# Four graph layers on one core: in layers 1 and 3 the edge work goes by tile with its results kept in a ring for the per-slot sums; in layer 0 the record fields are loaded once

## The reference

```
L0: alpha = softmax over the edges of a src of leaky(s_i[src] + s_j[dst]); sum alpha * (x W)[src] by dst
L1: g = attr64 @ Wdesc.T;  agg_i = sum over edges of node i=src of g * ssp(x Wj.T)[dst]
    m = ssp(x Wi.T) + agg; three residual MLPs, u*x + (...), two more residual MLPs
L2: z = relu(layernorm(x[src] @ top + x[dst] @ bottom)) * weight; mean by dst; gated update
L3: W = ssp(attr50 @ w1.T + b1) @ w2.T + b2, times a cosine cutoff C
    agg_i = sum over edges of node i=src of W*C * (x lin1.T)[dst];  x = x + ssp(agg @ lin2.T + b)
```

## Time and profile before

| | |
|---|---|
| median of the runs | 6994.6 us |
| profiled execution: span, its own time | 8544.4 us; the profile gives no second time for it |
| PE, DVE, ACT, POOL busy over the span | 4906.1, 4571.7, 2591.3, 4414.8 us |
| l0d, l1e, l3e in the profiled execution | 1363.7, 1400.5, 1434.9 us |
| DMA | 541.31 MB, mean 63 GB/s |

### The profile page before, as it was taken

The page is one execution under the profiler, slowest core; times in us unless marked ns, Lnnn a source line. Parts: engine busy times, 40 slices in busy tenths (PEclk is TensorE's granted clock), DMA queues, the critical chain, the costliest instruction groups (busy, mean ns, idle before and its releaser), DMA issues. The chain is left out here.

```text
span 8544.4 us, 129169 instructions
## 1 busy us (share of the span) xinstructions
PE 4906.1 (57%) x25390; PEld 3718.7 (44%) x25391; DVE 4571.7 (54%) x14726; ACT 2591.3 (30%) x6676; POOL 4414.8 (52%) x4764
## 2 busy tenths in 40 slices
PE   6666666622444444663454545656666556777767
PEld 4444444411333333552443444234444444555554
DVE  8655555534444444664333334867667674555555
ACT  2333333301212223663000000833333343333333
POOL 0255555544666665555555555046666615555553
PEclk9866676755555556776656566878788876776776
DMA  1233333351111112442222222022222212222221
GB/s 51 69 102 102 102 104 103 100 45 36 48 48 48 48 48 75 117 101 49 59 61 59 58 59 55 0 57 65 64 65 65 64 33 58 54 54 55 54 54 43
DMA packets 858703, 541.31 MB, mean 63 GB/s; under 512 B 652277, under 2 KB 757577, under 8 KB 858185
## 3 DMA queue, kind: packets, MB, share of 16 engines
q1 hardware_dynamic: 710536, 239.88, 12.9%
q0 software_dynamic: 148032, 300.00, 12.9%
HBM read 411.68 MB, written 127.68 MB: 63 GB/s over the span
## 5 line engine op out<-in xcount | busy, mean ns | idle before, releaser
L1326 POOL DMA_INDIRECT l2e_rows<-l_rows,k_src_of x832 | 841.9, 1012 | 749.8 <-POOLq L215 329.7
L1326 POOL DMA_INDIRECT spare<-l_rows,k_dst_of x832 | 804.9, 967 | 742.2 <-DVE l3e_prod L2313 311.5
L813 POOL DMA_INDIRECT src_records<-sort_rec,sort_idx x784 | 761.4, 971 | 767.8 <-DVEq L706 515.3
L1326 POOL DMA_INDIRECT l1e_rows<-l_rows,k_dst_of x832 | 785.8, 944 | 641.1 <-issue 296.7
L1193 POOL DMA_INDIRECT dst_rows<-l0d_out,l0d_idx x832 | 820.5, 986 | 466.7 <-issue 246.8
L866 DVE TENSOR_TENSOR acc<-acc,l1e_pR 128x128 f32 x832 | 238.6, 287 | 886.8 <-remote 703.5
L1494 PE MATMUL l1e_pG<-k_weights,l1e_dT 64*128 64x128 f32 x1664 | 233.7, 426 | 696.1 <-ACT l1e_dT L1514 412.0
L2247 PE MATMUL l3e_pH<-l3e_dT,k_weights 50*128 50x256 f32 x832 | 380.0, 549 | 341.0 <-DMA run_ml<-h_nodes 327.0
L2155 PE MATMUL l2e_pR<-l2e_z,l2e_oh 128*128 128x128 f32 x1664 | 301.0, 337 | 464.1 <-DVE acc L866 309.4
L1160 PE MATMUL l0d_pX<-table,l0d_ohT 128*128 x1664 | 448.9, 448 | 154.7 <-issue 71.2
L1494 PEld LDWEIGHTS l1e_pG<-k_weights,l1e_dT 64*128 64x128 f32 x1664 | 176.9, 292 | 771.4 <-issue 397.3
(11 more groups left out here) (413 smaller groups left out, 13714.8 us busy)
## 6 DMA issues: line engine op xcount, KB each, us to landing
sort_rows<-lo_rows SPq DMA_DIRECT2D x196, 256.0 KB
sort_rec<-rec SPq DMA_DIRECT2D x98, 472.0 KB
l0m_rows<-dst_rows SPq DMA_DIRECT2D x416, 66.0 KB, 2.1
l0m_rows<-dst_rows POOLq DMA_DIRECT2D x416, 66.0 KB
l1e_rec<-src_records SPq DMA_DIRECT2D x832, 32.0 KB
l2e_lrow<-dst_local SPq DMA_DIRECT2D x208, 128.0 KB
l3e_rec<-src_records SPq DMA_DIRECT2D x832, 25.0 KB
l0d_meta<-src_records SPq DMA_DIRECT2D x832, 6.0 KB
```

Of the source, the lines that this page charges most:

```text
L813: e.indirect_dma_start(kn.by_src_rec[:, :], bass.IndirectOffsetOnAxis(ap=r["idx"][:, st.quad, j:j + 1], axis=0), r["rec"][:, st.quad, j, : ...
L1326: e.indirect_dma_start(r["rows"][:, i % ring, j, 0:width], None, table[:, :], bass.IndirectOffsetOnAxis(ap=columns[:, i * G + j:i * G + j ...
```

## The change

- **l1e and l3e.** Gathers, record loads, products and all before them go by tile: `TSTEPS` = 196 steps instead of 208. `prod` becomes a ring of `KEEP` = 16 steps (64 tiles). Only the one-hots, the sum products and the additions still go by slot, in 208 steps; `add` on PE reads from the new table `kept_reg` which tile of the ring each slot wants. A stage can now have its own number of steps, and `run_steps` goes on with it after the others have ended.
- The four record loads of a step become one DMA of four tiles.
- The operands of the sum product change sides, so that its result is [node, feature]. l1e adds into `MT`, cleared at its start; mlp's first layer becomes a transposition on PE and an addition to `AC`. l3c is written anew: transpose `AC`, copy on ACT, product, bias, clamp, Exp, Ln, max, add, without the transposition back.
- **l0d.** SP loads the 12 fields of all 784 tiles in eight DMAs at the start into the arrays of sums (not in use yet); for each slot ACT copies its 12 values to `meta` (four small copies a step). `dst_of` is written once at the end, by tile, and the arrays of sums are cleared after it.
- Some small tiles move to other places in SBUF; the work in them stays.

The diff, cut to its core (`...` stands for what is left out):

```diff
+TSTEPS = T // G
+KEEP = 16
@@ run_steps
+    total = max(t[1] + (t[3] if len(t) > 3 else n) for t in stages)
...
-    for r in range(n, n + lag):
+    for r in range(n, total):
         one(r)
+def wait_tiles(eng, sem, st):
+    eng.wait_ge(sem, min(st.i + 1, TSTEPS) if isinstance(st.i, int) else st.i + 1)
@@ offsets
+            ch(e.tensor_scalar(kn.kept_reg[:, :], kn.slot_reg[:, :], KEEP * G - 1, None, ALU.bitwise_and))
@@ add_stages, hot_stages
-    return [(stage(j), lag) for j in range(G)]
+    return [(stage(j), lag, 1, STEPS) for j in range(G)]
@@ l0_messages: sync
-                tiles = slot_values(kn, e, kn.slot_regs["sync"], st, 64)
-                wait_step(e, r["msg_ok"], st, RING)
-                for j in range(G):
-                    e.dma_start(r["meta"][:, st.ring, j, :], kn.by_src_rec[bass.ds(tiles[j] * P, P), CM:CM + META]
-                                ).then_inc(r[f"ld{st.ring}"], 16)
+            for c in range(8):
+                e.dma_start(fields[:, c * part:(c + 1) * part, :], rows[:, c * part:(c + 1) * part, CM:CM + META]
+                            ).then_inc(r[f"ld{c}"], 16)
+            ready = [(c + 1) * part // G for c in range(7)] + [STEPS]
+            for c in range(8):
+                e.wait_ge(r[f"ld{c}"], 16)
+                e.sem_inc(r["loaded"], ready[c] - (ready[c - 1] if c else 0))
@@ l0_messages: vector
-            ch(e.memset(kn.sums0[:, :], 0.0))
-            ch(e.memset(kn.odd[:, :], 0.0))
...
-                ch(e.tensor_copy(kn.dst_of[:, slots], meta[:, :, 4]))
...
+            ch(e.tensor_copy(kn.dst_of[:, :], fields[:, :, 4]))
+            ch.wait()
+            ch(e.memset(kn.both[:, :], 0.0))
@@ l0_messages: scalar
+            def meta(st):
+                tiles = slot_values(kn, e, kn.slot_regs["scalar"], st, 64)
+                wait_step(e, r["loaded"], st)
+                wait_step(e, r["msg_ok"], st, RING)
+                for j in range(G):
+                    ins = e.activation(r["meta"][:, st.ring, j, :], whole[:, bass.ds(tiles[j] * META, META)], ACT.Copy)
+                ins.then_inc(r["meta_ok"], 1)
+            run_steps(e, ch, [(meta, 0), (exp, 5), (rows, 3), (copy, 1)], STEPS, RING)
@@ soft_layers (mlp's first layer has w == "turn")
+                    for j in range(GROUPS):
+                        ins = e.transpose(r["p"][:, m % 4, j // 4, (j % 4) * P:(j % 4 + 1) * P],
+                                          lay.src[:, GROUPS * (i % NW) + j, :], kn.ident[:, :])
@@ load_records
+        e.dma_start(r["rec"][:, st.quad, :, 0:width], rows[:, bass.ds(st.i * G, G), column:column + width]
+                    ).then_inc(r[f"ld{st.quad}"], 16)
+def kept_tile(r, at):
+    return r["prod"][:, bass.ds(at * P, P)]
+def kept_step(r, st):
+    return r["prod"][:, bass.ds((st.i % KEEP) * (G * P), G * P)]
+def kept_values(kn, e, st):
+    regs = kn.slot_regs["tensor"]
+    e.load(regs, kn.kept_reg[64:65, bass.ds(st.i * G, G)])
+    return [e.snap(g, min_val=0, max_val=KEEP * G - 1) for g in regs]
@@ l1_edges (l3_edges alike: 196 steps, add and hot with 208)
             def add(st):
+                kept = kept_values(kn, e, st)
                 wait_step(e, r["hot"], st)
-                wait_step(e, r["prod_ok"], st)
+                wait_tiles(e, r["prod_ok"], st)
                 wait_step(e, r["added"], st, 2)
                 for j in range(G):
-                    ins = e.matmul(r["pR"][:, st.par, j, :], r["prod"][:, st.par, j, :], r["oh"][:, st.par, j, :],
+                    ins = e.matmul(r["pR"][:, st.par, j, :], r["oh"][:, st.par, j, :], kept_tile(r, kept[j]),
                                    start=True, stop=True)
-            run_steps(e, ch, [(mults, 1), (add, 3), (turn_rec, 0)], STEPS, QUAD)
+            run_steps(e, ch, [(mults, 1), (add, 3, 1, STEPS), (turn_rec, 0)], TSTEPS, QUAD)
...
-                wait_step(e, r["summed"], st, 2)
+                wait_step(e, r["summed"], st, 4)
...
-            run_steps(e, ch, in_turn(add_stages(kn, e, ch, r, 1, 6), hot_stages(kn, e, ch, r, 1, 4, 2, 2))
-                      + [(prod, 4)], STEPS, RING)
+            ch(e.memset(kn.MT[:, :, :], 0.0))
+            ch.wait()
+            run_steps(e, ch, in_turn(add_stages(kn, e, ch, r, 1, 6, kn.MT), hot_stages(kn, e, ch, r, 1, 4, 2, 2))
+                      + [(prod, 4)], TSTEPS, RING)
@@ l3_finish (new vector order; its other engines follow it)
+            for k in range(GROUPS + 3):
+                if k < GROUPS:
+                    keep(k)
+                if 0 < k <= GROUPS:
+                    bias(k - 1)
+                if 1 < k < GROUPS + 2:
+                    smooth(k - 2)
+                if 0 < k <= GROUPS:
+                    clamp(k - 1)
+                if k > 2:
+                    add(k - 3)
```

More of the change, by code:

```diff
@@ L104, in one @@
             c, size = r - t[1], (t[2] if len(t) > 2 else 1)
-            if c % size or (k is None and not 0 <= c < n):
+            if c % size or (k is None and not 0 <= c < (t[3] if len(t) > 3 else n)):
                 continue
@@ L113, in one @@
                                       i % 4, i % RING, (unroll // RING) * k + i // RING))
-            t[0](steps if len(t) > 2 else steps[0])
+            t[0](steps if size > 1 else steps[0])
     if n < first + 2 * unroll:
-        for r in range(n + lag):
+        for r in range(total):
             one(r)
@@ L864, in add @@
                 ch.until(last[0])
-            acc = block(kn, kn.AC, blocks[j])
+            acc = block(kn, into, blocks[j])
             ins = e.tensor_tensor(acc, acc, r["pR"][:, st.par, j, :], ALU.add)
@@ L1099, in local_a @@
             def local_a(st):
[L1100 removed]
+                wait_step(e, r["meta_ok"], st)
                 slots, meta = bass.ds(st.i * G, G), r["meta"][:, st.ring, :, :]
@@ L1316, in l0_sums, with gather_rows @@
                     + [f"{m}{j}" for m in ("ld", "ld_first") for j in range(RING)])
-def gather_rows(kn, e, r, table, width, columns, used, ring=4):
-    for i in range(STEPS):
+def gather_rows(kn, e, r, table, width, columns, used, ring=4, steps=STEPS):
+    for i in range(steps):
         if i >= ring:
@@ L1651, in build @@
     def build(r):
+        small, at = spare[:, 7 * SLOTS:], 0
+        for name, size in (("none", NB), ("less", 1), ("log_var", NB), ("std0", NB), ("shift0", NB), ("mv0", 2 * NB)):
+            r[name] = small[:, at:at + size]
+            at += size
+        r["mv0"] = r["mv0"].rearrange("p (b c) -> p b c", c=2)
         def pick(name, k):
@@ L2401, in scalar @@
                 if k < GROUPS:
-                    e.wait_ge(r["clamped"], k + 1)
-                    ch(e.activation(r["part"][:, k % 2, :, :], r["part"][:, k % 2, :, :], ACT.Exp))
-                if k < GROUPS:
+                    for q in halves(k):
+                        e.wait_ge(r["turned"], q + 1)
+                        if q > 3:
+                            e.wait_ge(r["product"], q - 3)
+                        e.activation(r["T"][:, q % 4, 0:len(members(q)), :], four(r["pA"], q), ACT.Copy
+                                     ).then_inc(r["copied"], 1)
+                if k:
+                    e.wait_ge(r["clamped"], k)
+                    t = r["part"][:, (k - 1) % 2, :, :]
+                    ch(e.activation(t, t, ACT.Exp))
                     ch.wait()
-                    e.activation(r["part"][:, k % 2, :, :], r["part"][:, k % 2, :, :], ACT.Ln, bias=kn.half1[:, 0:1], scale=0.5
-                                 ).then_inc(r["logged"], 1)
+                    e.activation(t, t, ACT.Ln, bias=kn.half1[:, 0:1], scale=0.5).then_inc(r["logged"], 1)
         def sync(e, ch):
```

213 lines of the change are left out of this document (120 added, 93 removed).

## The result

The changed kernel takes 6907.5 us (median of four runs, 6904.3 to 6909.5) against 6994.2 of the kernel before in the same set of runs: 0.988 of it, 95% interval [0.9868, 0.9892], or 86.7 us faster. The forecast was 6933, the range 6875 to 6980.

The account below looks back on a forecast made before the run. POOL's indirect DMAs, one per 1.25 us, were taken to bound the five long stages in timed runs. Terms -64.8 + 8 - 7 + 2 + 0.6 = -61.2 us bring the median 6994.6 to 6933 us, range 6875 to 6980.

Parts of the forecast that it names:

- mlp: First layer as 49 transposes, seven additions and seven more Relus on ACT: +8 us, between 5 and 12.
- l3c: New order with five DVE passes per group, 5.4 us instead of 7.72: -7 us, between -15 and +5.
- l0d: Eight bulk field loads, 50 to 60 us, only the first eighth needed early: +2 us for sharing DMA engines, 0 to 10.
- all else: The +0.6 us term: offsets for kept_reg, one pass over 832 columns.
- What bounds: POOL's indirect DMAs, 1.25 us each and 5.0 per step of four, set the five long stages in timed runs.
- 1549.8 us: Profiled execution 8544.4 us less median 6994.6; almost all put down to POOL's waits, which sum to 1516.5 us.
- Edges by tile: l1e and l3e: 48 gathers fewer save 60.0 us each, 12 uncovered sum steps cost 27.6; both gain 64.8 us.
- S: Price of one step of sums alone at the end of l1e and l3e, taken as 2.3 us, near l0m's 2.34.
- lower bound of 1.8: Price from below of a step of sums alone, by DVE's busy time in l1e: 1.8 us.
- rival of the tail: l1e and l3e: sum-only steps form a chain of 5.0 us, not 2.3; 65 us come back, 6998 us; chance 0.08.
- Loads and ring: l1e and l3e: one record load per step and the ring of 16 steps change nothing, POOL covering the loads.
- rival of ACT: l0d: an ACT step exceeds POOL's 5.0 us, each 0.1 above costing 20.8 us; 7037 at 5.5; chance 0.07.

Follow-up runs that it names:

- e12: Kernel before with l1e and l3e gathers as plain DMAs (wrong rows), each followed by an iota: l1e 1327, l3e 1330, all other stages 4887.0 us.
- e4: The changed kernel run again unaltered, with a profile: 8458 us against 8513 of the kernel before, ratio 0.9925 [0.9901, 0.9949].

## Why the prediction was right, point by point

| | forecast | measured |
|---|---|---|
| l1e and l3e together | -64.8 | 2100.8 to 2036.5: -64.3 |
| mlp | +8 | 202.3 to 212.0: +9.7 |
| l3c | -7 (-15 to +5) | 58.1 to 43.1: -15.0 |
| l0d | +2 (0 to 10) | 1149.5 to 1146.5: -3.0 |
| l2e | 0 | 1115.0 to 1100.4: -14.6 |
| sort | 0 | 1063.4 to 1060.5: -2.9 |
| all else | +0.6 | +5.0, the rest |
| sum | -61.2 | 6989.4 to 6904.3: -85.1 |

"Measured" is e12's execution with the one run beside it against the profile after: one execution each, taken at different times. The rest of +5.0 is l0m, which isn't changed (482.6 against 487.9 us), so a stage can differ by 5 us without cause in the kernel. That -64.3 agrees with -64.8 to half a us is therefore luck; from the rhythm, starts and drains of e12's section it would be 2102.8 to 2036.5, -66.3.

- **What bounds.** Right that the 1549.8 us are POOL's waits and absent from the timed runs, and that POOL's 1.25 us set the stages: l1e is 784 of them and a tail. Wrong was the reason given, "the issue of small DMAs is slow and holds the stages": a kernel with a fourth of the loads (e4) is held alike, and there it is PE's signals that come up to 32 us late. It did no harm because the sum priced the gathers by POOL's rhythm where it isn't waiting, and that is the same in both conditions (1.25 us); that the timed runs would be the unheld ones was inferred from the median, and rightly. But the forecast for the profile ("from 8544 to about 7700") rested on it, and missed: 6904 in one condition and 8461 in the other.
- **Edges by tile.** 48 x 1.25 = 60 less, as forecast. S, taken from l0m as 2.3, is 2.09 in l1e, between that and the lower bound of 1.8, and paced by DVE as that bound has it, with 0.3 us of each step in which DVE waits too. The whole end of the stage, 33.7 and 34.6 us against 6.8 and 6.7 by slot, is 26.9 and 27.9 longer, the 27.6 of the sum. Twelve steps at 2.09 us would be 25.1; where the other 2 to 3 us lie isn't traced. The rival of the tail at 5.0 us per step falls.
- **Loads and ring.** Nothing, as forecast (e12: 2100.8 us against 2102.8 by POOL's rhythm, starts and drains). `kept_values` cost nothing that can be seen: POOL waits 1.2 us in all of l3e.
- **mlp.** Seven Relus more (42 for 35, 1.03 us each; ACT is busy 187.0 us where it was 180.4), as forecast. The other 3 us may be the later start; no run shows it by itself.
- **l3c.** The mechanism was right, the size too small: a group went from 7.72 us to 4.6, since the clamp of 896 columns takes 0.62 us, not the 1.08 at which I priced every pass, and the passes of two groups leave no gap. From the timeline of DVE, the first addition of two groups (4.60 us apart) and a clamp between them:

```profile
6875.08 1.08 DVE L2452 TENSOR_TENSOR x_nodes<-x_nodes,both 128x896 f32<-128x896 f32 x1
...
6878.14 0.62 DVE L2465 TENSOR_SCALAR l3c_part<-spare 128x896 f32<-128x896 f32 x1
...
6879.68 1.08 DVE L2452 TENSOR_TENSOR x_nodes<-x_nodes,both 128x896 f32<-128x896 f32 x1
```

- **l0d.** "Only the first eighth of the fields is needed" was wrong: SP gives the first signal after it has issued all eight, and their issue takes 61.24 us, a little over the estimate of 50 to 60. The first copy on ACT starts at 1598.0, 62.0 us into the stage, and the first scatter is 5.7 us later than in e12 (84.25 against 78.54). Against that the scatters themselves come at a mean of 1264.6 ns instead of 1274.9, 8.6 us in all; part of it may be the chip. The rival of ACT falls: four copies of 0.209 us fit and ACT waits 691 us for DVE before the exponent (in the earlier trace rows, 395.3 of the 942.8 us of wait there were "issue"). The groups of ACT in l0d:

```profile
L1207 ACT ACTIVATE spare<-both 128x12 f32 x832 | 107.4, 209 | 99.0 <-SPq L1077 97.1 <-issue 0.4
L1190 ACT ACTIVATE l0d_a<-l0d_a 128x16 f32<-128x16 f32 x208 | 44.8, 216 | 691.1 <-DVE l0d_a L1143 691.1
```

- **What the sum missed.** Of the 24 us between -61.2 and -85.1, l3c gives 8, shown by its timeline, and l0d 5, of which the scatters' pace gives more than all and may be the chip. 14.6 are l2e's, in which the work is unchanged and only small tiles moved. Its DMAs took 1011 ns in e12 and 994 in the profile after, which is 14 us over 832. Whether that is the chip or the placement stays open: the median DMA there is 955 against 944 ns and the shortest 948 against 940, which speaks for the chip for 7 to 9 us of it. So more than half of the gain beyond the forecast isn't explained by the change. Why PE's signals come late in the held runs also stays open; it comes with POOL's indirect DMAs, and no run tells more.

## What to carry to other kernels

When the profiled execution is longer than the timed ones, first find the engine whose rhythm has no waits in it and add up its waits by stage: if they make up the difference, price the change by the rhythm alone, and don't name a culprit until one run has taken it away and the trace has been asked whose signal came late. Work done once for each unit instead of once for each visit saves its share of the pacing engine, less the tail that the remaining work leaves at the end with nothing over it; that tail costs its own slowest engine (here DVE, 2.09 us per step), not the stage's rhythm. After this change DVE and PE are next at 4.1 us per step of l3e, so in l3e fewer gathers can bring some 22% of the stage at most (1022.5 to 800 us).

## What the runs showed of the hardware

- The same kernel ran at 6990 or at 8520 us, on five chips with one set of runs each, and never changed within a set. In the longer condition only stages with POOL's indirect DMAs are longer (sort by 40%, l1e and l3e by 34 to 36%, l0d by 21%, l2e by 17%). In l1e 308 of 729 of PE's signals come more than 2 us after their product's start (none above 0.44 us in the other condition), and ACT, DVE and in the end POOL wait for them, while the gathers land as fast as ever (2.20 against 2.22 us). Stages with plain DMAs at 90 to 129 GB/s are not touched.
- An indirect DMA of 128 rows costs POOL 0.94 us and 0.30 of issue in l1e, a plain one of the same bytes 0.53 to 0.55: l1e with plain DMAs takes 600 us instead of 1014.
- PE's granted clock in l3e is 0.68 held (e4), 0.81 not held and 0.96 without indirect gathers, with the same products: what differs is how long PE waits between them.
